# Row-by-row fetches in a graph-attention kernel: twelve chunks of unit 117 on SyncE in both attention passes, nine of unit 118 on ScalarE in the first

## What is computed

```python
def _gat(x, src, dst, W, att_src, att_dst, bias, n):
    xw = (x @ W).reshape(n, H, D)
    a_src = jnp.einsum('nhc,hc->nh', xw, att_src)
    a_dst = jnp.einsum('nhc,hc->nh', xw, att_dst)
    logits = jax.nn.leaky_relu(a_src[src] + a_dst[dst], NEG_SLOPE)
    m = jax.ops.segment_max(logits, dst, num_segments=n)
    ex = jnp.exp(logits - m[dst])
    s = jax.ops.segment_sum(ex, dst, num_segments=n)
    alpha = ex / (s[dst] + EPS)
    msg = xw[src] * alpha[..., None]
    out = jax.ops.segment_sum(msg, dst, num_segments=n)
    return out.mean(axis=1) + bias
...
src, dst = (edge_index[0], edge_index[1])
h = jax.nn.relu(_gat(x, src, dst, W1, ...) + (x @ lW1 + lb1))
out = _gat(h, src, dst, W2, ...) + (h @ lW2 + lb2)
...
# third layer
ef = jnp.concatenate([features[src], features[dst]], axis=-1)
att = jax.nn.relu(ef @ W_lin.T + b_lin)
...
new_features = jax.ops.segment_sum(alpha * ef, dst, num_segments=n_nodes)
```

## Time and profile before

| | |
|---|---|
| median of 3 runs | 5917.31 us (5913.04 to 5919.56) |
| the profiled execution | 5923.14 us, of which the span of its instructions is 5921.3 us |
| busy, share of the span | Pool 75%, TensorE matmul 66%, VectorE 62%, ScalarE 50% |
| the chain that ended last | Pool 70%, "issue" 24%, everything else 6% |
| mean DMA share of the 16 engines | 20 to 30% in passes 0 and 1, 30% in pass 2 |
| granted TensorE clock | 0.605 of full speed |

### The profile page before, as it was taken

How to read it: one execution, slowest core, us unless ns; L and a number is a source line. 1 busy time by engine, 2 the same in 40 slices (tenths; PEclk the granted TensorE clock), 3 DMA queues, 4 the chain that set the end, 5 groups by cost and what they waited for, 6 DMA issues and landing times.

```text
span 5921.3 us, 94392 instructions
## 1 busy us (share of the span) xinstructions
PE 3916.7 (66%) x22163; PEld 3603.6 (61%) x22163; DVE 3698.7 (62%) x9532; ACT 2971.8 (50%) x5708; POOL 4430.4 (75%) x4683
## 2 busy tenths in 40 slices
PE   5755555555556666666666666667777777777776
PEld 5655555555555555555555555567777777777776
DVE  5544444444445655555555555568888888888888
ACT  3433333333334355555555555556666666666665
POOL 7777777777777777777777777767777777777775
PEclk7656666655666656665555556666555555555556
DMA  7322222222223232322322222333333333333332
GB/s 168 81 63 63 64 64 63 63 63 63 60 62 69 59 68 67 66 67 67 67 67 67 67 66 65 66 77 91 89 90 89 86 90 90 90 89 90 90 90 67
DMA packets 334163, 447.03 MB, mean 75 GB/s; under 512 B 143370, under 2 KB 235602, under 8 KB 333372
## 3 DMA queue, kind: packets, MB, share of 16 engines
q0 software_dynamic: 149536, 217.14, 18.2%
q10 hardware_dynamic: 25824, 132.87, 7.1%
q1 hardware_dynamic: 158588, 94.96, 6.2%
HBM read 408.54 MB, written 40.09 MB: 76 GB/s over the span
## 4 chain that ended last, share of the span: by engine, by line
POOL 70%; issue 24%; PE 2%; DVE 2%; ACT 1%; POOLq 1%; DMA 1%; SPq 0%; DVEq 0%; ACTq 0%
POOL rows L1193 70%; PE psum L2318 1%; SPq L966 0%; DMA tab<-x_tab 0%; DVE mix L1529 0%; PE psum L2330 0%; ACT away L1889 0%; ACT L1932 0%; DMA w_heads<-in_L_gnn_W 0%; POOLq L1177 0%; ACT L1936 0%; PE psum L2260 0%; POOLq L1185 0%; DVE psum L1444 0%; DMA tab<-row_end 0%
## 5 line engine op out<-in xcount | busy, mean ns | idle before, releaser
L1193 POOL DMA_INDIRECT rows<-tab,idx_now x4623 | 4375.5, 946 | 1439.2 <-issue 1407.7
L2318 PE MATMUL psum<-share,rows 128*65 128x76 f32 (+10 forms) x6204 | 1164.5, 379 | 0.4 <-DVE share L1509 0.4
L1444 DVE TENSOR_TENSOR_SCAN psum<-cut,psum 48x224 f32<-48x224 bf16 (+3 forms) x524 | 450.4, 882 | 1076.8 <-PE psum L2290 1060.5
L2318 PEld LDWEIGHTS psum<-share,rows 128*65 128x65 f32 x6204 | 1080.7, 222 | 5.8 <-DVE share L1509 0.5
L2290 PE MATMUL psum<-ident,strip 128*48 128x128 f32 (+1 forms) x786 | 207.1, 400 | 1012.3 <-ACT strip L1923 1012.0
L2445 PE MATMUL psum<-own,hot_t 112*128 112x64 f32 x3126 | 646.5, 399 | 314.3 <-DVE mix L1716 311.8
L2445 PEld LDWEIGHTS psum<-own,hot_t 112*128 112x128 f32 x3126 | 624.9, 308 | 339.0 <-issue 242.8
L2290 PEld LDWEIGHTS psum<-ident,strip 128*48 128x48 f32 (+1 forms) x786 | 83.0, 132 | 1095.4 <-issue 1082.2
L2461 PE MATMUL psum<-hot,prob 128*128 128x112 f32 x3120 | 666.0, 408 | 5.0 <-DVE prob L1710 5.0
L2461 PEld LDWEIGHTS psum<-hot,prob 128*128 128x128 f32 x3120 | 647.2, 319 | 5.2 <-DVE prob L1710 5.2
L1891 ACT ACTIVATE hot_t<-away,ones 112x1536 bf16<-112x1536 f32 (+2 forms) x393 | 616.2, 1568 | 12.8
(11 more groups left out here) (284 smaller groups left out, 5627.6 us busy)
## 6 DMA issues: line engine op xcount, KB each, us to landing
rel_t<-rel_row ACTq DMA_DIRECT2D x128, 672.0 KB
rows<-tab,idx_now POOLq DMA_INDIRECT x4623, 2.5
rel_t<-rel_runs ACTq DMA_DIRECT2D x64, 672.0 KB
side_room<-tab SPq DMA_DIRECT2D x2304, 0.3 KB
own<-tab SPq DMA_DIRECT2D x262, 63.0 KB
cut<-cut_row SPq DMA_DIRECT2D x130, 120.2 KB
tab<-row SPq DMA_DIRECT2D x130, 112.0 KB
tab<-row SPq DMA_DIRECT2D x130, 63.0 KB
```

What stands on the lines that cost most here:

```text
L1193: nc.gpsimd.indirect_dma_start(rows_of[p][:, G * c.s + j, 0:D] if raw else rows_of[p][:, G * c.s + j, :], None, x if raw else halves[p], b ...
L1444: done = nc.vector.tensor_tensor_scan(running, cuts[:, 0:-1], values, NEG, ALU.add, ALU.max)
L2318: done = nc.tensor.matmul(summed[:, :, LO[j]:HI[j]], chunk_rows(c, j)[:, 0:D + 1], of[:, j, :, 0:SUBS[j]], start=not opened, stop=j == chu ...
```

## The change

`SIDE` becomes 117. In passes 0 and 1 all twelve chunks of unit 117 are fetched by SP row by row (1536 rows a pass). In pass 0 alone nine chunks of unit 118 are fetched by ScalarE in the same way (1152 rows). Unit 123 is gathered by Pool again. Pool's gathers so fall by twelve in pass 0 and by three in pass 1.

SP's stretch becomes four loops of four turns (units 6 to 101), sixteen rows a unit; units 102 to 113 follow in a loop without such rows. ScalarE's new fetches stand at the end of each iteration of units 6 to 113, ten or eleven rows a unit, in two loops of nine turns. On all engines the loop of a pass loses its last turn: units 114 to 130 are now written out.

The semaphores get new names since two of them are shared, and `chunk_rows`, `beside` and `sums_of` take the pass. The branches for pass 2 (`SIDES[2]` = 0) add nothing to the program.

```diff
-    SIDE, SIDES, SIDE_W = NU - 8, 9, 71
-    SIDE_LOOPS = 2
-    SIDE_TURNS = (NU - RING) // RING // SIDE_LOOPS - (1 if SIDE_LOOPS == 2 else 0)
+    SIDE = NU - 14
+    SIDES, SIDE_W = (12, 12, 0), (71, 71, 131)
+    SIDE_LOOPS, SIDE_TURNS = (4, 4, 1), (4, 4, 0)
+    ACT_SIDES, ACT_LOOPS, ACT_TURNS = 9, 2, 9
+    ASIDE = (SIDES[0] + ACT_SIDES, SIDES[1], SIDES[2])
...
+    LOOPED = (NU - RING) // RING - 2
...
-            with eng.Fori(1, (NU - RING) // RING) as q:
+            with eng.Fori(1, 1 + LOOPED) as q:
...
             def fetch_side_rows(p, c, h):
-                t0, t1 = [SIDE_STEP * (c.s + i) // RING for i in range(2)]
+                block, each = P // SIDE_LOOPS[p], SIDES[p] // SIDE_TURNS[p]
+                turn = c.q - 1 - SIDE_TURNS[p] * h
+                t0, t1 = [each * block * (c.s + i) // RING for i in range(2)]
...
-                    if p < 2 and beside(c) == G:
+                    if p < 2 and beside(p, c) == G:
                         pool.wait_ge(sums_ready, n - RING + 2)
                         pool.sem_inc(go, 1)
-                    for j in range(beside(c) if p < 2 else 0, chunks(c)):
+                    for j in range(beside(p, c), chunks(c)):
...
+            def fetch_side_rows(c, h):
+
+                block = P // ACT_LOOPS
+                turn = c.q - 1 - ACT_TURNS * h
+                t0, t1 = [block * (c.s + i) // RING for i in range(2)]
+                _, nodes = nc.values_load_multi_w_load_instructions(act_home[h:h + 1, bass.ds(block * turn + t0, t1 - t0)],
+                                                                    engines=(act.engine,))
+                for t, node in zip(range(t0, t1), nodes):
+                    r = block * h + t
+                    act.dma_start(side_rows[0][r:r + 1, bass.ds(turn + SIDES[0], 1), 0:SIDE_W[0]].rearrange("p a w -> p (a w)"),
+                                  tab[0][bass.ds(node, 1), HALF:HALF + SIDE_W[0]]).then_inc(rel_aside_in, 16)
...
+                if beside(p, c.plus(1)) > beside(p, c):
+                    act.wait_ge(side_in[p], side_before[p] + 16 * P * SIDES[p])
+                    if p == 0:
+                        act.wait_ge(rel_aside_in, 48 + 16 * P * ACT_SIDES)
...
-                for c in units(act, TAIL):
+                for c, h in units_aside() if p == 0 else ((c, None) for c in units(act, TAIL)):
...
+                    if h is not None:
+                        fetch_side_rows(c, h)
```

More of the change, by code:

```diff
@@ L131, in came_aside @@
     def came_aside(p, c, count):
-        return sum(count(min(SIDES - G * i, G)) for before in range(2) for i in range(-(-SIDES // G))
+        return sum(count(min(ASIDE[before] - G * i, G), 2 if before == 2 else 1)
+                   for before in range(3) for i in range(-(-ASIDE[before] // G))
                    if (SIDE + i) % RING == c.s and (before < p or before == p and c.at_least(SIDE + i)))
     def first_landed(p, c):
-        return landed(p, c, 1, 1, 2, 2) - 16 * came_aside(p, c, lambda m: 1)
+        return landed(p, c, 1, 1, 2, 2) - 16 * came_aside(p, c, lambda m, first: first)
     def rest_landed(p, c):
-        return landed(p, c, G - 1, LASTC - 1, G - 2, LASTC - 2) - 16 * came_aside(p, c, lambda m: m - 1)
+        return landed(p, c, G - 1, LASTC - 1, G - 2, LASTC - 2) - 16 * came_aside(p, c, lambda m, first: m - first)
     def chunks(c):
@@ L1084, in units_aside @@
+                    at_w = HALF if p < 2 else 4 * D - SIDE_W[p]
+                    sp.dma_start(row, tab[p][bass.ds(node, 1), at_w:at_w + SIDE_W[p]]).then_inc(side_in[p], 16)
+            def units_aside(p):
                 for u in range(RING):
                     yield unit(u), None
-                for h in range(SIDE_LOOPS):
-                    with sp.Fori(1 + SIDE_TURNS * h, 1 + SIDE_TURNS * (h + 1)) as q:
+                for h in range(SIDE_LOOPS[p]):
+                    with sp.Fori(1 + SIDE_TURNS[p] * h, 1 + SIDE_TURNS[p] * (h + 1)) as q:
@@ L1111, in _ @@
                 fetch_cuts(p, unit(2))
-                for c, h in units_aside() if p < 2 else ((c, None) for c in units(sp)):
+                for c, h in units_aside(p) if SIDES[p] else ((c, None) for c in units(sp)):
                     n = NU * p + c.u
@@ L1860, in stage_indices, with units_aside @@
                     .then_inc(idx_staged, 1)
+            def fetch_side_rows(c, h):
[8 more added lines that the diff above has]
+                                  tab[0][bass.ds(node, 1), HALF:HALF + SIDE_W[0]]).then_inc(rel_aside_in, 16)
+            def units_aside():
+                for u in range(RING):
+                    yield unit(u), None
+                for h in range(ACT_LOOPS):
+                    with act.Fori(1 + ACT_TURNS * h, 1 + ACT_TURNS * (h + 1)) as q:
+                        for s in range(RING):
+                            yield Unit(q, s), h
+                for u in range(RING * (1 + LOOPED), TAIL):
+                    yield unit(u), None
             def stage_early(p):
@@ L1912, in strip_of @@
                     act.sem_inc(strip_ready, 1)
-                b = beside(c)
+                b = beside(p, c)
                 if b > 0:
                     first = G * (c.u - SIDE)
-                    copied = nc.scalar.activation(strip[:, 1:b + 1, :], side_rows[:, first:first + b, heads_of], ACT.Copy)
+                    copied = nc.scalar.activation(strip[:, 1:b + 1, :], side_rows[p][:, first:first + b, heads_of], ACT.Copy)
                 if b < m:
```

156 lines of the change are left out of this document (90 added, 66 removed).

## The result

The changed kernel takes 5889.12 us (median of five runs, 5888.13 to 5892.48), the kernel before 5917.31 (five runs, 5913.04 to 5919.56). The ratio is 0.9955, with a 95% interval of 0.9941 to 0.997. That is 28.2 us less, where the prediction has 27.9. Two of its terms were wrong, though, and the same comparison on another chip has the opposite sign (e5).

What follows compares the result with a forecast made beforehand. Pool's gathers at 1.25 us each were taken as the bound, with waits at the pass seams. 15.0 + 3.75 + 6.9 + 2.3 = 27.9 us less gave 5889.4 us, 0.47% faster, range 5884 to 5904.

Steps and rivals of the forecast that it cites:

- Part 1: Pool's gathers: twelve fewer in pass 0 save 15.0 us, three fewer in pass 1 save 3.75; loop ends add 2.3.
- The 2.3 us for the loop ends: Pool's loop, one turn fewer in each pass: saves the surplus gap of 0.70, 0.81 and 0.75 us, together 2.3.
- Part 2: Seam after pass 1: the earlier jump lets late strips recover, Pool's wait falls from 13.96 to about 7.1, saving 6.9 us.
- Part 3: SyncE's queue in pass 1: with the added rows a unit takes 14.4 us, below 15.0, hidden under Pool's gathers.
- rival C: SyncE becomes the bound of passes 0 and 1 if loads of sixteen cost 3.5 us: +30 us, 5919; chance 5%.
- The pairs: SyncE's register loads: 0.22 us for each pair where the count is even, each number where odd; sixteen cost 1.8 us.
- Part 4: ScalarE's row fetches in pass 0: a turn takes 86.1 us, 89.1 with a stall, hidden under Pool's 90.06.
- the reserve: Pass 0: consumers may lag 48 us before Pool stops, 2.7 us in each of 18 turns.
- the jump of 26.3 us: Pass 0, twelve and nine chunks fetched aside: consumers gain 6.4 us a unit and have recovered by unit 122.
- rival A: ScalarE becomes the bound of pass 0, two queues sharing the descriptor generator: up to +72 us, 5961; chance 15% in all.

Runs made afterwards that it cites:

- e5: The changed kernel with no edit, on another chip, against the kernel before there: 8260.0 us against 7770.8, ratio 1.0624.
- e9: No rows fetched aside by SyncE or ScalarE, all units gathered by GpSimd, against the kernel before: 5931.76 us against 5916.64, ratio 1.0024.
- e6: The changed kernel with ScalarE fetching 10, 12, 10, 10, 12, 10 rows a unit instead of 10, 11, 11, 10, 11, 11: 8227.1 us, ratio to before 1.0595.
- e10: Only ScalarE's nine chunks in pass 0 fetched aside, none by SyncE, against the kernel before: 5919.79 us, ratio 1.001.
- e1: The kernel before with no edit, run as a second copy against itself: 7591.5 us against 7590.2, ratio 1.0003.
- e2: The kernel before with SyncE's nine chunks taken from unit 117 instead of 123 and shorter loops, no ScalarE fetches: 7615.8 us, ratio 1.0029.
- e11: The kernel before with nine chunks at unit 117 and shorter loops, repeated on a third slower chip: 7614.43 us against 7596.15, ratio 1.0022.
- e4: The changed kernel without ScalarE's fetches, twelve chunks by SyncE in passes 0 and 1, against the kernel before: 8009.3 us, ratio 1.0544.
- e12: The changed kernel plus eight chunks of unit 117 by SyncE in pass 2, against the kernel before: 8214.31 us, ratio 1.0806.

## Why the prediction was right, and where it was wrong

**Part 1, the gathers: right, with one term that was nothing.** 4623 to 4608 gathers of 0.944 us and 0.30 behind each: 18.75 us. e9 shows the price from the other side. The 2.3 us for the loop ends were wrong. The chain's "1.00 issue" of the earlier trace rows was read as a gap of 1.00 in place of 0.30. But the longest "issue" wait of a gather in the kernel before is 0.3 us, among 4662 (the waits above), and the starts of the gathers stand at most 1.26 us apart inside pass 0, loop ends included. The chain of before in order of time, around the first of the two marks:

```profile
901.47 0.18 POOL rows L1193
...
901.72 1.00 issue
902.72 0.94 POOL rows L1193
```

The two gathers start 1.25 us apart, as everywhere. The "1.00 issue" is the rest of the first gather and the usual 0.30 us, put down to another name, and no lost time. The term is 0.

**Part 2, the seam: right in kind, a little too large.** The schedule was borne out: strip 117 is copied at 3716.69, 118 at 3728.32, 119 at 3739.96, 120 at 3751.64, steps of 11.6 to 11.7, and 121 waits for its rows again. The wait fell from 13.96 to 8.61 in place of 7.1, and the wait for `row_end` from 4.9 to 4.4, which the prediction hadn't looked at: together 5.9 of the 6.9 us. The microsecond that is missing isn't in the strips:

```profile
3884.57 0.20 ACT L1969 ACTIVATE strip<-rows 128x4 f32<-128x4 f32 x1 [0.61 <-DMA rows<-tab,idx_now]
3884.68 0.23 ACT L1978 ACTIVATE strip<-rows 128x48 f32<-128x48 f32 x1
...
3892.67 0.40 SPq L1072 DMA_DIRECT2D tab<-row  x1
```

Strip 129 is copied as soon as its rows have landed, since its first piece waited for them: on time, as forecast. What the prediction took as fixed is the way from there to the first gather of pass 2: 9.3 us before, 10.75 now (3895.43 - 3884.68), since the row is stored 8.0 us after the strip in place of 6.5 (before: 3923.01 - 3916.49). Why it is stored later is open. In e9, where strip 129 is on time as well, the way is 9.6 us and the waits are 7.48 and 3.63, 1.9 us less together than in the changed kernel. The seam after pass 0 was taken as unchanged: its first wait rose by 1.2 us and its second fell by 1.8, 0.5 less together.

**Part 3, SyncE: right, for a wrong reason.** Sixteen numbers take 1.14 us, below both the 1.8 chosen and the 3.5 of rival C. The pairs were a misreading: e6 shows that the place of the first number decides. The Trainium skill (Runtime: NRT & Kernel Launch, Instruction fetch mechanics) puts such loads at about 200 ns a register; the loads of ten to twelve from other places come near (0.22 to 0.24 us a number), the sixteen in 1.14 us don't, and the measurement decides. Counted as in the prediction, SyncE's unit in pass 1 is 12.4 us from the store at 2601.43 to the end of the cut at 2613.85, and 0.6 more: 13.0, where 13.9 was forecast. The turn's end costs 2.9 us (2627.07 to 2629.95), forecast 3. So rival C couldn't come in on that chip. But a turn's end doesn't cost this in every loop: in the trace of before SyncE's next DMA comes 2.9 to 3.2 us after the last row in its first loop of pass 0 and 0.7 in its second (at the turn that starts at 1047.24, `cut` is issued at 1052.87, the last row ends at 1052.10), and ScalarE's first loop shows 0.5 (above). The bodies have the same number of fetches; what decides isn't shown.

**Part 4, ScalarE: right.** Units with eleven rows take 15.05 us (forecast 14.9), with ten 13.2 to 13.5 (13.2). A turn takes 87.3 us in the first of its two loops and 90.2 in the second, where each turn end stalls for 3 us; the forecast has 86.1 without the stall and 89.1 with it. Half of the 1.2 us that is missing in the sum is the load of eleven, 2.59 on this queue against 2.43 on SyncE's, 4 x 0.16 = 0.6 a turn. GpSimd's turn takes 89.9. So ScalarE is 0.3 us a turn over GpSimd's pace in the second loop, which the reserve takes up: the strips stand 26.6 us behind their rows at unit 8 (21.1 before), 14.2 at 40 and 2 to 5 from 60 on. Of the 48 us of reserve 21 were never used, and GpSimd never stopped for it. After the jump of 26.3 us the strips have caught up with their rows at unit 120, where 122 was forecast. That two queues of single rows disturb each other was the mechanism of rival A. It doesn't: a row takes ScalarE 244 ns in the median beside SyncE's rows and 244 without them (e10), and SyncE 238 ns beside ScalarE's (pass 0) and 237 without them (pass 1). The period is 0.44 to 0.47 us on both, below the 0.50 from which rival A decides. Of the lock on the generator that the Trainium skill names (Perfetto Trace Analysis, DMA Instruction — HWDGE) no cost shows here.

**The sum.** In the two profiled executions the difference is 34.5 us: 18.75 gathers, 5.9 and 0.5 at the seams, 0.8 lost at the start of pass 0, and some 10 us because the gathers of this execution of after stand 1.2486 us apart (mean) and those of before 1.2508. That pace isn't an effect of the change: e9, with no rows aside at all, has 1.2494, and e10 1.2485. It moves from one execution to the next (e1, and e2 against e11). What the change gives by its own terms is 18.75 + 5.9 + 0.5 - 0.8 = 24.4 us, the medians say 28.2, and the interval of the ratio is 18 to 35. So the near hit of 27.9 is in part luck: 2.3 us of it were nothing, 1.0 too much for the seam, and the measurement can't tell 24 from 28.

**What the prediction didn't see** is the condition under which all of it holds. On three chips met here GpSimd isn't the bound, 31 to 43% of the chain is SyncE's queue, and the change, timed on one of them, costs 6%; its variants e4 and e12 cost 5 and 8% on the other two. The trace of before, taken on one chip, couldn't show that. What it did show is that the change's work goes on queues with little slack: by the prediction 0.6 us a unit on SyncE and 1 to 4 us a turn on ScalarE.

## What to carry over

Count the bound in units of its instruction (here 1.25 us a gather) and the seams in late strips; both terms held (e9, where the jumps and the fetches are gone, shows them from the other side). A term read from the chain of waits has to be checked against the spacing of the instructions themselves: the 2.3 us for loop ends would have fallen at once. And work that is taken off the bound and put as many small instructions on queues with little slack is a gain only while those queues keep their pace: where the instructions of such a queue are now and then held for 0.7 or 1.4 us, 0.45% gained turned into 6% lost, so such a change should be timed on more than one chip.

## What the runs showed of the hardware

- The same kernel takes 5917 us on some chips and 7590 to 7771 on others, with gathers and scans equally long (gather 944 ns, scan 882 ns in the changed kernel and in e1). What differs first is the queue that issues many small DMAs: in e1 SyncE's instructions, register moves as well as DMA issues, are held 4242 times for 0.70 or 1.40 us, ScalarE's never; in e5, where ScalarE fetches rows in pass 0, ScalarE's are held 683 times there. What holds them wasn't found.
- A load of several registers costs by where its first number stands as well as by how many it has: ten or sixteen in 1.1 to 1.2 us from starts at multiples of 16; on ScalarE's queue ten in 2.38, eleven in 2.59 and twelve in 2.80 from other starts (0.23 to 0.24 us each), on SyncE's eleven in 2.43.
- Single-row fetches on two queues at once don't slow each other measurably: 244 ns on ScalarE's with and without SyncE's beside them (the changed kernel and e10), 238 and 237 on SyncE's with and without ScalarE's, at 0.44 to 0.47 us from one to the next.
- A turn's end costs SyncE and ScalarE about 3 us in some loops and 0.5 to 0.7 in others of the same body, and GpSimd nothing that its gathers show.
- A long run of equal gathers keeps a pace of 1.248 us in some executions and 1.251 in others, and both on one chip and with one kernel: 10 us over 4600 gathers.
